# Joining a step of scores with a step of turned scores on four row strips of TensorE, and letting an expert's adds go unordered

## What is computed

```python
x = x + _L0_xattn_ref(ctx, ctx, _layernorm(x), ...)   # part A: one head of width 256
x = x + _L0_ffn_ref(_layernorm(x), ...)               # part B: 32 heads of width 8, then a GELU feed-forward
x = x + _L1_xattn_ref(_layernorm(x), ctx, ...)        # part C: one head, a self score added
x = x + _L1_ffn_ref(_layernorm(x), ...)               # part D: 16 heads of width 16, then a routed feed-forward
```

```python
att = jnp.einsum('bqhd,bkhd->bhqk', q, k) / np.float32(np.sqrt(hd))
p = jax.nn.softmax(att, axis=-1)
o = jnp.einsum('bhqk,bkhd->bqhd', p, v)
```

```python
buf = buf.at[top1, s1].set(x, mode='drop')
buf = buf.at[top2, s2].set(x, mode='drop')
h = jax.nn.relu(jnp.einsum('ecd,edf->ecf', buf, w1) + b1[:, None, :])
y = (jnp.einsum('ecf,efd->ecd', h, w2) + b2[:, None, :]) * (1.0 - MOE_TOKEN_DROPOUT)
return g1[:, None] * y1 + g2[:, None] * y2
```

## Time and profile before

| | us |
|---|---|
| three runs | 2140.34, 2146.3, 2147.84 |
| median | 2146.3 |
| the profiled execution, its time | 2144.83 |
| its span, first to last instruction | 2143.0 |
| PE busy | 1926.4 (90% of the span) |
| DVE busy | 1365.2 (64%) |
| ACT busy | 998.2 (47%) |
| POOL busy | 585.5 (27%) |

### The profile page before, as it was taken

The page is one execution under the profiler, slowest core; times in us unless marked ns, Lnnn a source line. Parts: engine busy times, 40 slices in busy tenths (PEclk is TensorE's granted clock), DMA queues, the critical chain, the costliest instruction groups (busy, mean ns, idle before and its releaser), DMA issues. The chain is left out here.

```text
span 2143.0 us, 37582 instructions
## 1 busy us (share of the span) xinstructions
PE 1926.4 (90%) x13601; PEld 1447.2 (68%) x13601; DVE 1365.2 (64%) x3573; ACT 998.2 (47%) x1958; POOL 585.5 (27%) x475
## 2 busy tenths in 40 slices
PE   4689999999999999999999999997878649999996
PEld 3456666666766666676666667665656439989986
DVE  2436667676666767676676767666775557676663
ACT  1244555555555555556555555653424223333331
POOL 1102031212303121221313122130111146677773
PEclk9679999999999999999999999997878759999998
DMA  5222443515143351514335251423120253534332
GB/s 184 84 84 77 133 150 107 168 48 168 63 158 119 116 173 64 168 63 158 105 111 167 89 167 63 149 85 115 43 89 1 79 171 81 125 87 85 48 50 23
DMA packets 205704, 225.79 MB, mean 105 GB/s; under 512 B 14168, under 2 KB 195248, under 8 KB 205520
## 3 DMA queue, kind: packets, MB, share of 16 engines
q1 hardware_dynamic: 191136, 206.40, 29.3%
q0 software_dynamic: 14384, 16.99, 5.0%
HBM read 150.82 MB, written 72.52 MB: 104 GB/s over the span
## 5 line engine op out<-in xcount | busy, mean ns | idle before, releaser
L1218 DVE TENSOR_REDUCE MX<-bank 128x2 f32<-128x512 f32 x768 | 493.6, 684 | 171.4 <-PE bank L851 169.8
L1467 ACT ACTIVATE PT<-bank 128x512 f32<-128x512 f32 x768 | 416.7, 597 | 253.2 <-PE bank L888 250.7
L851 PE MATMUL bank<-KS,QS 32*128 32x256 f32 (+1 forms) x1536 | 198.0, 337 | 44.2 <-DVE MX L1218 43.6
L888 PE MATMUL bank<-QM,KS 32*128 32x256 f32 (+1 forms) x1536 | 197.4, 336 | 37.8 <-ACT PT L1467 27.3
L903 PE MATMUL bank<-PT,VA 128*32 128x256 f32 x3072 | 214.2, 398 | 8.5 <-ACT PT L1467 7.5
L851 PEld LDWEIGHTS bank<-KS,QS 32*128 32x128 f32 (+1 forms) x1536 | 120.4, 193 | 132.7 <-DVE MX L1218 70.9
L888 PEld LDWEIGHTS bank<-QM,KS 32*128 32x128 f32 (+1 forms) x1536 | 121.1, 193 | 125.3 <-issue 66.8
L1819 ACT ACTIVATE hid<-bank,b1T 128x512 f32<-128x512 f32 x128 | 87.8, 686 | 231.1 <-PE bank L1771 231.1
L703 POOL TENSOR_TENSOR rrB<-uwB,cst 128x4 f32<-128x4 f32 x16 | 16.3, 1018 | 595.5 <-DVE uwB L1187 595.5
L1784 PE MATMUL bank<-W2h,hTh 128*128 128x256 f32 x512 | 144.0, 281 | 0.0
L1784 PE MATMUL bank<-W2l,hTh 128*128 128x256 f32 x512 | 142.7, 279 | 0.0
(11 more groups left out here) (323 smaller groups left out, 3778.4 us busy)
## 6 DMA issues: line engine op xcount, KB each, us to landing
W<-in_L_ffn_w_dram SPq DMA_DIRECT2D x48, 1024.0 KB, 7.4
KS<-k_dram SPq DMA_DIRECT2D x64, 512.0 KB, 5.8
QS<-q_dram SPq DMA_DIRECT2D x64, 512.0 KB, 6.0
k_dram<-qTQ SPq DMA_DIRECT2D x32, 256.0 KB, 2.5
q_dram<-pTQ SPq DMA_DIRECT2D x32, 256.0 KB, 7.3
k_dram<-PRP SPq DMA_DIRECT2D x32, 256.0 KB, 2.5
q_dram<-cTP SPq DMA_DIRECT2D x32, 256.0 KB, 2.6
X<-in_x_dram SPq DMA_DIRECT2D x16, 256.0 KB, 6.5
```

The costliest lines, as they stand in the source:

```text
L851: x = mm(halves(u)[:, r, :], Q[strip, slot, r * P:(r + 1) * P], K[strip, slot, :], start=True, stop=True)
L888: x = mm(halves(2 + u)[:, kc, :], K[strip, slot, kc * P:(kc + 1) * P], QM[strip, slot // 2 % 2, slot % 2, :], start=True, stop=True)
L1218: v.tensor_reduce(MX[:, slot % 4, j, :], halves(u), AX, ALU.max, negate=True).then_inc(h.maxed, 1)
L1467: s_.activation(PT[:, n % 8, :, :], halves(2 + n % 2), ACT.Exp, scale=h.scale).then_inc(h.exp, 1)
```

## The change

A new step X (`crossed`) does one S step and one E step of the heads of width 8 together. The two are five steps apart (`LEAD`), so their strips never meet: where S has p = 1, E has p = 0. The 8 products go out in turn, two of the scores and two of the turned scores, twice. X stands behind both waits, that for the maxima and that for the exponentials, and behind that for `QM`. The first 5 S steps and the last 5 E steps of `h0` stay single, 11 of each become X. DVE and ACT do what they did, in the places of the letter X. All four strings are written anew. The heads of width 16 keep their steps.

In the experts the wait ahead of each add goes. POOL waits for all earlier adds only before the first add of an expert. Two semaphores by the parity of the unit take the place of one, DVE waits on them before it writes a gate and `yo` again, and empty places are left out of the transfer (`oob_is_err=False`) instead of going to padding rows.

```diff
-N_SCORE, N_TURN, N_EXP, N_VALUE, N_LIN2, N_LIN1 = 24, 8, 24, 12, 28, 19
+LEAD = 5
+N_SCORE, N_TURN, N_EXP, N_CROSS, N_VALUE, N_LIN2, N_LIN1 = 8 + LEAD, 8, 8 + LEAD, 16 - LEAD, 12, 28, 19
-ORDER = "QQPPSQPPSQSTPSPESTEPSEVETSVESQESPTSQPSEVSPQSPESPTSQPVSEPQSEPSPEVQTESPQPESVEPPSEQVPSQETPSQEPQEVPSQEVPQTEPEPVEPEQEVQV"
+ORDER = "QQSPQPSPPSQTSEPSETPSEVEPTSEQESVPSQTPSEQSVPSPESTQPVXPQXPXPQVPTXQPPXVXPXPQVPTXQPXPXVQPVQPXQPETPQEPEVEQEVQV"
+            def crossed(h, b, prev):
+                K, Q, R = KS[h.width], QS[h.width], h.rows
+                base = {n: now(t, b * v) for n, v in dict(head=h.heads, two=h.twos).items()}
+                for (slot, p), (far, q) in zip(h.steps, h.steps[LEAD:]):
+                    assert q == 1 - p
+                    n, m = slot * h.nh + 2 * p, far * h.nh + 2 * q
+                    for c in range(DC):
+                        if (far, q) == (c * h.slots // DC, 0):
+                            t.wait_ge(s_stack[h.width, c], b * STACKED + STACKED)
+                    t.wait_ge(h.maxed, base["head"] + m)
+                    if (slot % 2, p) == (0, 0):
+                        t.wait_ge(h.shifted, base["two"] + (slot // 2 + 1))
+                    if n:
+                        t.wait_ge(h.exp, base["head"] + n)
+                    elif prev:
+                        t.wait_ge(prev[0].exp, prev[1] * prev[0].heads + prev[0].heads)
+                    for k in range(2):
+                        for u in range(2):
+                            strip = slice((2 * q + u) * R, (2 * q + u + 1) * R)
+                            x = mm(halves(u)[:, k, :], Q[strip, far, k * P:(k + 1) * P], K[strip, far, :], start=True, stop=True)
+                            if k == 1:
+                                x.then_inc(h.scored, 1)
+                        for u in range(2):
+                            strip = slice((2 * p + u) * R, (2 * p + u + 1) * R)
+                            x = mm(halves(2 + u)[:, k, :], K[strip, slot, k * P:(k + 1) * P], QM[strip, slot // 2 % 2, slot % 2, :], start=True, stop=True)
+                            if k == 1:
+                                x.then_inc(h.st, 1)
+                    yield
-                return {"S": chain(scores(h1, r - 2, hd[1]) if hd else idle(8), scores(h0, r, hb[1]) if hb else idle(16)),
+                return {"S": chain(scores(h1, r - 2, hd[1], ALL) if hd else idle(8), scores(h0, r, hb[1], slice(0, LEAD)) if hb else idle(LEAD)),
+                        "X": crossed(h0, r, hb[1]) if hb else idle(N_CROSS),
-                        "E": chain(exps(h1, r - 2, hd[1]) if hd else idle(8), exps(h0, r, hb[1]) if hb else idle(16)),
+                        "E": chain(exps(h1, r - 2, hd[1], ALL) if hd else idle(8), exps(h0, r, hb[1], slice(16 - LEAD, 16)) if hb else idle(LEAD)),
...
                     g.wait_ge(s_yv, n + 1)
-                    g.wait_ge(s_add, n * 16 + 16)
-                    if r == 0:
-                        g.sem_inc(s_adding, 1)
+                    if r == 0 and u % NH == 0 and u:
+                        for i in range(2):
+                            g.wait_ge(s_add[i], u // 2 * 16 * HT4)
                     g.indirect_dma_start(out=out, out_offset=bass.IndirectOffsetOnAxis(ap=put[:, n:n + 1], axis=0),
                                          in_=yo[u % 2][:, r, :], in_offset=None,
-                                         bounds_check=T + P - 1, oob_is_err=True, compute_op=ALU.add).then_inc(s_add, 16)
+                                         bounds_check=T - 1, oob_is_err=False, compute_op=ALU.add).then_inc(s_add[u % 2], 16)
...
                 v.wait_ge(s_gg[b], nth_of(u) * 16 * HT4)
-                v.wait_ge(s_adding, u + 1)
+                if u >= 2:
+                    v.wait_ge(s_add[b], u // 2 * 16 * HT4)
```

More of the change, by code:

```diff
@@ L84, in __init__ @@
         self.heads = D // width
+        self.steps = list(product_of(range(self.slots), range(self.pairs)))
         self.groups = self.heads // 4
@@ L833, in _, with scores @@
                 events.start(t)
-            def scores(h, b, prev):
+            def scores(h, b, prev, steps):
                 K, Q, R = KS[h.width], QS[h.width], h.rows
                 base = now(t, b * h.heads)
-                for slot, p in product_of(range(h.slots), range(h.pairs)):
+                for slot, p in h.steps[steps]:
                     n = slot * h.nh + 2 * p
@@ L871, in turns, with exps @@
                     yield
-            def exps(h, b, prev):
+            def exps(h, b, prev, steps):
                 K, R = KS[h.width], h.rows
                 base = {n: now(t, b * v) for n, v in dict(head=h.heads, two=h.twos).items()}
-                for slot, p in product_of(range(h.slots), range(h.pairs)):
+                for slot, p in h.steps[steps]:
                     n = slot * h.nh + 2 * p
@@ L1203, in rest, with maxima @@
                 x.then_inc(*dve[part].tick(n + "l"))
-            def maxima(h, b, prev):
+            def maxima(h, b, prev, steps):
                 base = {n: now(v, b * k) for n, k in dict(head=h.heads, two=h.twos).items()}
-                for slot, p in product_of(range(h.slots), range(h.pairs)):
+                for slot, p in h.steps[steps]:
                     two = slot // 2
@@ L1456, in take_cols, with exps @@
                 x.then_inc(*act[part].tick(tick))
-            def exps(h, b, prev):
+            def exps(h, b, prev, steps):
                 base = {n: now(s_, b * k) for n, k in dict(head=h.heads, group=h.groups).items()}
-                for n in range(h.heads):
+                for n in range(h.heads)[2 * steps.start:2 * steps.stop]:
                     s_.wait_ge(h.st, base["head"] + (n + 1))
@@ L1652, in experts @@
         s_x0 = [sem(f"s_x0{r}") for r in range(HT4)]
-        s_meta, s_yb, s_add, s_adding = sem("s_meta"), sem("s_yb"), sem("s_add"), sem("s_adding")
+        s_meta, s_yb, s_pad, s_add = sem("s_meta"), sem("s_yb"), sem("s_pad"), [sem(f"s_add{i}") for i in range(2)]
         block = stack.enter_context(nc.Block())
@@ L1689, in _ @@
                 sp.wait_ge(s_w[i], 32 * (NE // 2))
[L1690 removed]
+            sp.wait_ge(s_pad, 16)
+            for i in range(2):
+                sp.wait_ge(s_add[i], UNITS // 2 * 16 * HT4)
         @block.gpsimd
         def _(g):
[L1695 removed]
+            g.dma_start(out[T:T + P, :], cst[:, 0:D]).then_inc(s_pad, 16)
             def gather(src, dst, u, r, done):
```

21 lines of the change are left out of this document (11 added, 10 removed).

## The result

| | before | after |
|---|---|---|
| median of four runs each, us | 2146.7 | 2186.0 |
| ratio, with its 95% interval | 1 | 1.0183 (1.0158 to 1.0208) |
| the profiled execution: time, span | 2144.83, 2143.0 | 2187.98, 2186.2 |

The change makes the kernel slower by 1.8%, some 40 us. I had forecast 2107, faster. The span is 43.2 longer in the profiled executions, and PE's timeline splits this at three products: the self score of the third and of the fourteenth round that have one (eleven rounds apart, all full), and the first product of the experts.

What follows compares the result with a forecast made beforehand. PE was taken to bound the full rounds and the experts. Savings of 30 us in 13 rounds, 3 in three others and 8 at the end, with allowances for run median and unseen coupling, gave 2107, range 2086 to 2132.

Steps and rivals of the forecast that it cites:

- Nothing is added on DVE, ACT, POOL or SP in a round. They only change places.: In the rounds: the work of these four engines stays the same, so the saving on PE gets no addition from them.
- Wrong if the granted clock falls in full rounds: A sign against the forecast: PE's granted clock, 1.00 in the full rounds before, would fall there.
- PE's work: PE in a full round: 3.2 us less, 2.6 from strip steps and 0.6 from six fewer changes of mode.
- Added waits: PE in a full round: new waits at the self score (0.3) and part C's norm (0.6), together 0.9 us.
- The two X behind V and behind the self score: Around the self score: these X come short by about 0.35 and 0.4 us, net +0.3 in a round.
- the two reductions that hid POOL's power: Ahead of part C's norm: their cover of 1.28 us is lost, half of it, 0.6, taken as wait.
- second rival: DVE takes over the saving: full where X are dense, so PE only waits; 2138, or 2121 with half gone; chance 0.22.
- slower rival: The joined wait in each X lets each engine's delay stop the other; slower by over 0.5%, up to 2168; chance 0.06.
- The experts' adds: At the kernel's end: without the wait the last add starts 8.0 us sooner, at least 4.2 of it left.
- The late rounds: `LATE` and `LAST`, which have no X, only another letter order: no change, 4 us either way for the range.
- With half of it gone 2121: A milder case of DVE taking over the saving: half of the 3.2 us in a round lost, total 2121.
- the first rival: No new waits: 3.2 us for 13 rounds, 2 for three, 8 at the end, 56 off, 2091; chance 0.15.

Runs made afterwards that it cites:

- h_early: The changed kernel with POOL's step of `H`, `H` and `RES` one letter earlier, ahead of the power for part D1; 2139.5 us, ratio 0.996.
- split: The changed kernel with each X as a step S and a step E behind it, each with its own wait; 2187.0 us, ratio 1.018.
- split_early: h_early with each X as a step S and a step E behind it, each with its own wait; 2142.8 us, ratio 0.998.
- tail: The kernel before with only the change to the experts' adds, its rounds left as they were; 2142.7 us, ratio 0.996.
- h_late_before: The kernel before with POOL's step of `H`, `H` and `RES` one letter later, behind the power for part D1; 2184.7 us, ratio 1.016.
- slow_power: tune with POOL's power for part D1 raised in three instructions instead of one; 2161.9 us, ratio 1.006.
- tune: h_early with one X of the full rounds, behind the self score, moved behind the next product; 2125.1 us, ratio 0.989.
- fill_early: h_early with extra PE transposes of `AOQ` and `NP` filling two waits around part C's norm; 2143.8 us, ratio 0.998.

## Why the prediction was wrong

**The step that failed** is "Nothing is added on DVE, ACT, POOL or SP in a round. They only change places." The places were the cost. I walked the new order on PE and on DVE beside part C, and never on POOL, where the power for D1 had moved ahead of `H`, `H` and `RES`. The letters show it: before, the step of POOL with `H` (the 14th Q) stood two letters ahead of the 23rd P with the power, and now it stands behind. That put POOL's three instructions beside `NP`: 2.0 of wait in each round, and 2.8 by the clock. Undone, 47 of the 79 us between 2107 and 2186 are back. Of the other 32, some 14 are the half clock left in the eleven rounds (95.5 against 94.2), and some 26 the 2.0 by which thirteen rounds save less than forecast, shown below. Against these, the round with the routing and the experts gained a few us more than I had taken.

**"Wrong if the granted clock falls in full rounds"** came true. I had named it as a sign and given it no rival and no price, though it is over half of the loss in a round.

**PE's work.** I had 3.2 less. In a round without half clock PE is busy 88.5, and 90.8 before: 2.35 less. X does take 0.44 (1172.85 to 1173.29 in the changed kernel). The strip steps gave what I had for them: summed from start to start over the two rounds, without the waits between, they take 18.4 before and 15.9 in h_early, 2.5 less for the forecast 2.6. (Both sums are some 1.1 above mine, since over half of the pairs that I priced at 0.67 take 0.8 to 1.0, in both kernels, some of them with no wait between.) What did not come is the 0.6 for six changes between strips and full array. The other products of the round take 0.25 more, and not 0.6 less.

**Added waits.** I had 0.9. PE's idle time in a round went from 3.7 (94.5 - 90.8) to 5.7 (94.2 - 88.5), so 2.0. The two X behind V and behind the self score came near: 0.55 and 0.36 (1172.85 and 1174.70 in the changed kernel) for the 0.35 and 0.4 named. Part C's norm did not: I took 0.6 for "the two reductions that hid POOL's power", on DVE. But the chain there doesn't lie on DVE's queue. It is the end of the last product, residual, moments, power, norm, 4.2 us, and what hides it is PE's own work between. A step S and a step E fewer stand there, and with `AOQ` now ahead of `NP`, ACT's copy of `nTP` lies open too: 0.68 and 0.69, and 0.61 ahead of the transposes of `MT`.

With both terms as measured a round gives 0.3 and not 2.3. Without the meeting on POOL that is close to the second rival's outcome, though not its reason. By the Trainium skill, in TensorEngine Tiling (Array Packing), Performance Considerations, PSUM Bottleneck, the engines that empty PSUM may become the bound, but DVE is idle for 30 us of a round in h_early. The saving went into chains across four engines and not into an engine that is full.

**The slower rival** had the right sign and the wrong mechanism: it wanted 3.7 us of new waits in a round from the joined wait. PE's idle time in a round did grow by 3.9 (98.7 - 91.1 = 7.6, from 3.7), but split has the same round, 98.9, without a joined wait, and split_early and h_early both have 95.5.

**What was right.** The experts' adds gave 8.0 at the end and 7.8 in the run tail, the last add starts 0.79 behind its `yo`, and the drain stays at 7.8. The late rounds, with the end of the one with the routing, got 2.6 longer (216.7 from the mark at 1539.2 before, 219.3 from 1586.4 after), inside the 4 that I allowed. The stretch ahead of them that I had taken for the round with the routing, 121.9 before, takes 115.9, so it gained 6.0 where I took 1.

**A sum that was off.** "With half of it gone 2121" does not follow: the first rival's rounds give 47.6, and half of that off 2138 is about 2114. The second rival thus overlaps the forecast more than I wrote. It changes nothing about the failed step.

## What to carry over

When a change rewrites an order that all engines walk, walk it on each engine, the idle ones above all. Ask which SBUF-only instructions of DVE and POOL now fall together. A stretch saved on a PE-bound path is only worth its full price where no chain across other engines starts and ends inside it, since PE's own work was the cover of that chain. And where PE's idle time grows, look at the granted clock before anything else: here it cost more than the waits themselves, and one product in the right gap gave back more than the joined steps.

## What the hardware showed that I had not expected

**DVE and POOL side by side.** A TENSOR_SCALAR of 128x256 from SBUF to SBUF on DVE takes 0.41 us alone and 1.35 (median of 32 in the changed kernel, up to 1.48) while POOL runs TENSOR_TENSOR instructions of 1.26 to 1.31 each. A small TENSOR_TENSOR of DVE with both inputs in SBUF (`MT` from `MX` and `MT`, 128x8) takes 1.27 instead of 0.17 in 13 cases of the changed kernel, each time behind the start of POOL's `YB` and as long as it. DVE's reductions, which read PSUM, keep their 0.68 beside POOL. Where DVE starts first it loses nothing and POOL does: in h_early `NP` starts 0.14 ahead of POOL's norm and takes 0.74, and POOL's norm takes 2.73, where two such instructions take 2.42 at their shortest. That fits the Trainium skill, SBUF — State Buffer, section "Who interferes with whom": DVE and GpSimd share one pair of ports, a DVE instruction such as tensor_scalar may take it for its whole length, and whichever comes first blocks the other. The trace agrees, in both orders. By that rule this change could have been forecast as slower, had I looked for the pair on POOL's queue.

**The clock.** PE's granted clock fell to half for 3.4 or 6.8 us at a time in or right behind waits of 0.4 to 2.2. The longest single wait doesn't decide it: a wait of 1.71 in h_late_before brought it down in 3 of 11 rounds, 0.92 in slow_power in 7, and 2.17 in the changed kernel in all 11. What else stands around a wait seems to play a part: in tune the falls at the self score went when a full product came between it and an X. Filling two waits by 0.4 each in fill_early left the sum at half clock as it was. What decides, these runs leave open.
